# Expert results written to token order by GpSimd, with the place carried in each row (four layers of attention and feed-forward)

## What is computed

```python
x = x + L0_xattn(layernorm(x), ctx, ...)   # convolved causal attention
x = x + L0_ffn(layernorm(x), ...)          # shared expert + 2 of 8 experts, gelu
x = x + L1_xattn(ctx, layernorm(x), ...)   # attention at sampled places
x = x + L1_ffn(layernorm(x), ...)          # 2 of 8 experts, silu gate
x = x + L2_xattn(layernorm(x), ctx, ...)   # cross attention
x = x + L2_ffn(layernorm(x), ...)          # 2 of 8 experts, relu
x = x + L3_xattn(layernorm(x), ctx, ...)   # cross attention
x = x + L3_ffn(layernorm(x), ...)          # product keys, 8 rows per token
```

```python
h = act(xf @ Wfc[e] + bfc[e]) @ Wproj[e] + bproj[e]
routed = routed + h * gate[:, e:e + 1]     # gate is 0 but for two experts a token
```

## Time and profile before

| | |
|---|---|
| median of 3 runs | 1910.25 us |
| the three runs | 1899.67, 1910.25, 1910.5 us |
| profiled execution, its own time | 1902.02 us |
| its span | 1900.3 us |
| busy TensorE, weight load | 1273.0 us (67%), 771.8 us (41%) |
| busy VectorE, ScalarE, GpSimd | 1026.5 (54%), 530.6 (28%), 565.7 us (30%) |
| mean granted TensorE clock | 0.754 |
| blocks of stage 0, 1, 2 | 647 to 740, 1094 to 1194, 1449 to 1543 us |

### The profile page before, as it was taken

One profiled execution on the slowest core, in us unless ns is written; L12 is line 12 of the kernel. 1 busy time (PEld: TensorE's weight loads), 2 busy tenths in 40 slices (PEclk: granted clock), 3 DMA queues, 4 the chain that ended last, 5 costly groups with the idle time before them and its releaser, 6 DMA issues. The chain is left out here.

```text
span 1900.3 us, 26101 instructions
## 1 busy us (share of the span) xinstructions
PE 1273.0 (67%) x9212; PEld 771.8 (41%) x9212; DVE 1026.5 (54%) x2918; ACT 530.6 (28%) x1053; POOL 565.7 (30%) x700
## 2 busy tenths in 40 slices
PE   1458878787884896455645399378876955787720
PEld 1223334343442785345645288222335842222210
DVE  2454455454553232599999655334433325547796
ACT  0123233332341452122312133023423522323310
POOL 6041222212334002541011600331132033155674
PEclk8588798887995998555555599669967978866665
DMA  5930000000003121433532111400001210022232
GB/s 135 389 136 1 1 1 1 1 1 0 12 7 105 41 67 48 119 100 92 136 93 61 34 60 62 130 23 1 12 18 49 67 49 23 2 63 64 79 98 74
DMA packets 73254, 116.48 MB, mean 61 GB/s; under 512 B 11565, under 2 KB 52320, under 8 KB 70624
## 3 DMA queue, kind: packets, MB, share of 16 engines
q1 hardware_dynamic: 60320, 85.24, 14.9%
q0 software_dynamic: 12800, 29.51, 5.4%
HBM read 77.03 MB, written 37.68 MB: 60 GB/s over the span
## 5 line engine op out<-in xcount | busy, mean ns | idle before, releaser
L1671 DVE CUSTOM_DVE_ANT_0 arena<-ps,far 128x512 f32<-128x512 f32 (+3 forms) x256 | 118.2, 488 | 108.6 <-PE ps L1345 107.7
L2002 POOL DMA_INDIRECT wide<-in_w_ud,arena x128 | 130.0, 1015 | 77.7 <-DVE arena L2033 40.7
L2922 PE MATMUL ps<-wide,arena 78*128 78x32 bf16 x3840 | 112.1, 187 | 51.6 <-ACT wide L3035 41.8
L1260 POOL TENSOR_SCALAR_AFFINE_SELECT arena<-arena 128x260 f32<-128x260 f32 (+1 forms) x128 | 53.7, 432 | 308.9 <-ACT arena L1538 308.8
L810 POOL DMA_INDIRECT arena<-ys_d,slot_i x64 | 61.2, 956 | 246.6 <-DMA ys_d<-arena 197.4
L2922 PEld LDWEIGHTS ps<-wide,arena 78*128 78x128 bf16 x3840 | 110.3, 104 | 58.9 <-ACT wide L3035 45.2
L983 PEld LDWEIGHTS ps<-arena 128*128 128x128 f32 (+1 forms) x1012 | 123.4, 192 | 4.0
L983 PE MATMUL ps<-arena 128*128 128x128 f32 (+1 forms) x1012 | 123.6, 275 | 0.0
L1538 ACT ACTIVATE arena<-ps 128x1024 f32<-128x1024 f32 (+1 forms) x96 | 84.6, 881 | 109.9 <-PE ps L1367 109.4
L1367 PE MATMUL ps<-arena 32*128 32x128 f32 (+3 forms) x512 | 114.2, 491 | 1.1 <-DVE arena L1690 1.1
L2543 DVE TENSOR_REDUCE arena<-ps 128x6 f32<-128x462 f32 (+1 forms) x96 | 54.9, 581 | 93.6 <-PE ps L2289 69.9
(11 more groups left out here) (498 smaller groups left out, 2632.4 us busy)
## 6 DMA issues: line engine op xcount, KB each, us to landing
arena<-low_d SPq DMA_DIRECT2D x32, 780.0 KB
xs_d<-zrow SPq DMA_DIRECT2D x1, 10240.0 KB, 30.1
ys_d<-zrow SPq DMA_DIRECT2D x1, 10240.0 KB, 55.9
arena<-xs_d SPq DMA_DIRECT2D x69, 128.0 KB, 2.0
ys_d<-arena SPq DMA_DIRECT2D x69, 128.0 KB, 1.7
arena<-in_w SPq DMA_DIRECT2D x2, 1408.0 KB
wide<-in_Wfc SPq DMA_DIRECT2D x1, 2048.0 KB, 11.8
wide<-in_Wproj SPq DMA_DIRECT2D x8, 256.0 KB, 6.5
```

The source lines that it names most:

```text
L1671: ins = nc.vector.tensor_tensor_reduce(junk[:, n % 2, 384 * i:384 * i + w], ps[:, n % 2, 384 * i:384 * i + w], far[:, T - w:T], 1.0, 3 * N ...
L2002: pool.indirect_dma_start(out=rows_g[t % 4][:, h, :], out_offset=None, in_=A["w_ud"], in_offset=bass.IndirectOffsetOnAxis(ap=eidi[:, t % 8 ...
L2922: mm = nc.tensor.matmul(ps[:, 2 * (i % 3) + h // 2, col:col + 4 * HD], ring[m_ % 4][:, h * NK + p_, t % 2 * P:t % 2 * P + P], table[n // 4 ...
```

## The change

Each row that goes to an expert gets a 129th value, the number of the DRAM row to which its result shall go: 2048 rows for the first choices and 2048 for the second, in token order, behind one row for each of the 5888 slots of the blocks, to which the results of empty slots go. Since the two choices of a token have different numbers, they need two sets of rows in SBUF: `rows` and `twins` (the gated stage had two already). VectorE writes the number's column and, in the plain stages, normalises each batch twice.

In the blocks SyncE no longer stores. VectorE computes from the loaded numbers of block i the targets `goal` (128x2, integer), at the head of result(i); it waits before that until the indirect writes of block i-2 have landed, since `goal` and `yb` have two buffers each. load(i) now waits for goal(i-3) besides turn(i-3). GpSimd waits for each result and writes it with two indirect DMAs of 128 rows (`results`) to `y_d`, which replaces `ys_d` and isn't filled with zeros.

Behind the blocks SyncE waits for all writes and loads the results of each batch with two plain DMAs of 256 KB (`summands`), the last batch's in `last_rows`; two pairs of buffers serve the four batches. VectorE's `combine` adds a batch at a time. The gathers are gone from GpSimd's order. The wide weights for stage 2 are loaded behind the last batch's results of stage 1.

```diff
+RW = D + 1
+TRASH = NBLK * BLK
+STAGE = 16384
 ...
-        ys_d = nc.dram_tensor("ys_d", (SLOTS, D), F32, kind="Internal").ap()
+        xs_d = nc.dram_tensor("xs_d", (SLOTS, RW), F32, kind="Internal").ap()
+        y_d = nc.dram_tensor("y_d", (TRASH + 2 * NTT * P, D), F32, kind="Internal").ap()
 ...
+                nc.vector.tensor_scalar(rows[b][:, :, D], token[:, tiles(b)], float(STAGE * n + NTT * P), None, ALU.add)
+                if not gated:
+                    nc.vector.tensor_scalar(twins[b][:, :, D], token[:, tiles(b)], float(STAGE * n), None, ALU.add)
+                    for t in range(NT):
+                        nc.vector.tensor_scalar(twins[b][:, t, 0:D], xa[:, NT * b + t, :], mv16[:, NT * b + t, 0:1],
+                                                rstd16[:, NT * b + t:NT * b + t + 1], ALU.subtract, ALU.mult)
 ...
                     if i >= 3:
                         sp.wait_ge(m["T"], i - 2)
+                        sp.wait_ge(m["goal"], i - 2)
                     sp.dma_start(xb[:, i % 3, :, :], xs_d[bass.ds(r, BLK), :].rearrange("(p c) d -> p c d", c=2))\
                         .then_inc(m[f"x{i % 3}"], 16)
-                def store(i):
 ...
+                for b in range(B - 1):
+                    summands(sp, b)
+
+            def summands(sp, b):
+                if b >= 2:
+                    sp.wait_ge(m["added"], b - 1)
+                for j in range(2):
+                    lo = TRASH + NTT * P * j + T * b
+                    sp.dma_start(yg[b % 2][j], y_d[lo:lo + T, :].rearrange("(t p) d -> p t d", p=P)).then_inc(m[f"ys{b % 2}"], 16)
+
+            def last_rows(sp):
+                summands(sp, B - 1)
 ...
-            def gather(pool, lo, hi):
-                for t in range(lo, hi):
-                    if t >= 4:
-                        pool.wait_ge(m["added"], t - 3)
-                    for j in range(2):
-                        pool.indirect_dma_start(out=yg[:, t % 4, j, :], out_offset=None, in_=ys_d,
+            def results(pool):
+                for i in range(NBLK):
+                    pool.wait_ge(m["y"], i + 1)
+                    for c in range(2):
+                        pool.indirect_dma_start(out=y_d, in_=yb[:, i % 2, c, :], in_offset=None,
+                                                out_offset=bass.IndirectOffsetOnAxis(ap=goal[:, i % 2, c:c + 1], axis=0))\
+                            .then_inc(landed[i % 2], 16)
 ...
                 def result(i, one):
+                    if i >= 2:
+                        dve.wait_ge(landed[i % 2], sent(i % 2, i // 2))
+                    dve.wait_ge(m[f"x{i % 3}"], 16 * (i // 3 + 1))
+                    nc.vector.scalar_tensor_tensor(goal[:, i % 2, :], xb[:, i % 3, :, D], float(-STAGE * n), trash[:, i, :], ALU.add, ALU.max).then_inc(m["goal"], 1)
                     dve.wait_ge(m["down"], i + 1)
-                    if i >= 2:
-                        dve.wait_ge(m[f"ys{i % 2}"], 16 * (i // 2))
 ...
             def combine(dve, ch, b):
-                for t in range(NT * b, NT * b + NT):
-                    added_to(dve, ch, t)
+                dve.wait_ge(m[f"ys{b % 2}"], 32 * (b // 2 + 1))
                 for j in range(2):
                     if gated:
-                        ins = nc.vector.tensor_tensor(xa[:, t, :], xa[:, t, :], yg[:, t % 4, j, :], ALU.add)
+                        ins = nc.vector.tensor_tensor(x_all[:, b, :, :], x_all[:, b, :, :], yg[b % 2][j], ALU.add)
 ...
                 blocks.settled(pool)
-                blocks.gather(pool, 0, 5)
                 rstd(0)
-                blocks.gather(pool, 5, 8)
 ...
                 rstd(1)
-                blocks.gather(pool, 8, 16)
```

More of the change, by code:

```diff
@@ L36 @@
 NEG = -1e30
-ARENA = 23104
+ARENA = 23500
 STOP = 99
@@ L588, in build @@
         at[0] = 14400
[L589 to L592, removed]
+        late_rows = [[carve(NT, D) for _ in range(2)]]
+        rows2 = [carve(NT, RW) for _ in range(B)]; turned2 = carve(T)
+        late_rows.append([carve(NT, D) for _ in range(2)])
@@ L623, in build, with routing @@
         xa = x_all[:, :, :, :].rearrange("p b t d -> p (b t) d")
-        def routing(n, rows, scaled, turned_to, place, bank, emptied, finished, reuse):
+        def routing(n, rows, twins, turned_to, place, bank, emptied, finished, reuse):
             gated = n == 1
@@ L655, in turn @@
                     pe.wait_ge(r["xn"], NT * b + t + 1)
[L656 removed]
+                    mm = nc.tensor.transpose(ps[:, k_, t * P:t * P + P], rows[b][:, t, 0:D], ident[:, :])
                 mm.then_inc(turn7, 1)
@@ L760, in scatter @@
                 for j in range(2):
-                    src = (scaled if gated and j == 0 else rows)[b]
+                    src = (twins if j == 0 else rows)[b]
                     pool.indirect_dma_start(out=xs_d, in_=src[:, t, :], in_offset=None,
@@ L1046, in emptied @@
                 return i + 1 - d, d
-            R_ = routing(n, rows, None, turned_to, place, bank, emptied, lambda dve, b: None,
+            R_ = routing(n, rows, twins, turned_to, place, bank, emptied, lambda dve, b: None,
                          lambda act, b: act.wait_ge(W["zero"], wcount["zero"]) if b == 3 else None)
@@ L1098, in route_all, with expert_stage @@
             clear_sems(attn_sems + list(r.values()))
-        def expert_stage(n, attention, rows, scaled):
+        def expert_stage(n, attention, rows, twins):
             blocks = moe(n)
@@ L1106, in _ @@
                     blocks.sync(sp)
-                    if parts.sync is not None:
-                        parts.sync(sp)
+                    parts.sync(sp)
                 @block.gpsimd
                 def _(pool):
-                    blocks.gpsimd(pool, rows, scaled)
+                    blocks.gpsimd(pool, rows, twins)
                     if parts.ahead_gpsimd is not None:
                         parts.ahead_gpsimd(pool)
+                    blocks.results(pool)
                     parts.gpsimd(pool, Chain(pool, pool_chain))
@@ L2177, in reuse @@
                     act.wait_ge(turn7, place["lg", b - 1] + 1)
-            R_ = routing(2, rows2, None, lambda b: turned2, place, bank, emptied, finished, reuse) if routes else None
+            R_ = routing(2, rows2, twins2, lambda b: turned2, place, bank, emptied, finished, reuse) if routes else None
             K_ = product_keys(place, emptied, finished) if keys_after else None
@@ L2191, in block_keys, with sync @@
                                         headmask[:, :].unsqueeze(2).to_broadcast([P, H, S2]), ALU.mult).then_inc(c["kbd"], 1)
+            def sync(sp):
+                blocks.last_rows(sp)
+                if keys_after:
+                    K_.store(sp)
             def gpsimd(pool, ch):
@@ L2752, in reuse @@
                 else:
-                    act.wait_ge(m["added"], NTT)
-            R_ = routing(1, rows1, scaled1, lambda b: turned1, place, bank, emptied, finished, reuse)
+                    act.wait_ge(m["added"], B)
+            R_ = routing(1, rows1, twins1, lambda b: turned1, place, bank, emptied, finished, reuse)
             def wrapped(eng, ch, b):
```

135 lines of the change are left out of this document (68 added, 67 removed).

## The result

| | before | after |
|---|---|---|
| median | 1904.97 us (4 runs, 1899.67 to 1910.5) | 1945.85 us (4 runs, 1940.39 to 1948.3) |
| profiled execution, its span | 1902.02, 1900.3 us | 1947.25, 1945.5 us |
| busy TensorE, VectorE, GpSimd | 1273.0, 1026.5, 565.7 us | 1312.4, 1048.5, 599.2 us |
| blocks of stage 0, 1, 2, first transpose to last result | 93.0, 99.2, 93.3 us | 97.9, 152.5, 98.1 us |

The changed kernel takes 1.021 times as long, 95% interval 1.0164 to 1.0257. The forecast of 1934 us lies 12 us under the median, which is inside its range. The medians lie 40.9 us apart. The span of the profiled executions grew by 45.2 us where the sum had 30.

A forecast was written before the change was run, and what follows sets the result against it. No engine was taken as full over the span; TensorE bounds the expert stages. Terms 45 + 5 + 7 - 9 - 18 = +30 us gave 1932 from the profiled 1902.0, adjusted to 1934 us, range 1900 to 1967.

The forecast's parts named there:

- The last step of the sum: From 1932 us, the profiled run plus 30, halfway toward runs whose median lies 8 us higher: forecast 1934 us.
- gated blocks: Gated stage: loads wait for places computed behind the third product; 6.4 us a block for 4.15, 20 blocks, +45 us.
- plain blocks: Plain stages: loads come later, behind the weight copies; 0.25 us per two blocks, +5 us, range 0 to 10.
- routing: Attentions before the stages: second set of rows and narrow operations on VectorE, +7 us, range 4 to 13.
- last result to first statistics: Behind each stage: write, two loads and sums replace the old tail; -9 us together, range -4 to -14.
- first to fourth statistics: Three attentions: third batch's norm no longer waits behind GpSimd's gathers; 7.0, 6.7 and 4.7 us go, -18 us.
- last stretch of the program: The forecast's sum had no term for this stretch, so 0.
- the rival, which the prediction had as a case apart: Gated stage: clock falls to its lower level, 2.8 us more in half of 20 blocks, +28 us: 1962; chance 0.18.
- the clock near 1: Sign of being right: gated stage's TensorE busy share falls to about 65% at a clock near 1.
- whether the copies would hold up GpSimd's writes: Plain stages: by the skill's rule some 0.9 us per block, about 2 us more each stage; left out of the sum.
- The writes' landing: Plain stages: rival where writes land only after 4 us and gate every block, some +10 us each: 1954; chance 0.06.
- "No change" as a rival: Start of three attentions: ending GpSimd's gathers relieves 43 us against costs of 57, time unchanged, 1920; chance 0.22.

The follow-up runs named there:

- the filler: Changed kernel plus seven unused identity transposes a gated block while TensorE waits for rows: 1935.68 us, ratio 1.0185 against the kernel before.
- the kernel with the same extra work alone: Kernel before, with VectorE normalising each batch's rows twice in the plain stages' routing: 1907.27 us, ratio 1.002; on another chip 1928.13 us, 1.0081.
- the order alone changed: Kernel before, with GpSimd computing batch 2's rstd ahead of the gathers of tiles 12 to 15 in both cross attentions: 1891.51 us, ratio 0.996.
- the places early: Changed kernel, with the places of block i+1 computed at the head of VectorE's round i, four buffers: 1876.48 us, ratio 0.9861 against the kernel before.

## Why the prediction was right, and where its terms were off

The direction, the mechanism and its place were right. Each line below is a stretch of the two profiled executions. The size came out by some luck: the costs were 26 us above the forecast, and the reliefs 11 above it, which hid part of that. The last step of the sum also has a slip: halfway between 1932 and 1940 lies 1936 and not 1934.

| term of the sum | forecast | profile |
|---|---|---|
| gated blocks, 99.2 to 152.5 us | +45 | +53.3 |
| plain blocks, 93.0 to 97.9 and 93.3 to 98.1 | +5 | +9.7 |
| routing, first attention 14.9, its end -0.6, sampled 1.3, first cross 4.8 | +7 | +20.4 |
| last result to first statistics, three times | -9 | -14.4 |
| first to fourth statistics, three times | -18 | -18.3 |
| last stretch of the program, 243.3 to 238.0 | 0 | -5.3 |
| sum | +30 | +45.4 |

(The span's difference is 45.2; the rest is rounding and the sampled attention's 48.2 to 48.1.)

- **Gated stage.** The chain was worked out at 6.4 us a block and takes 6.25, so the wait costs 20 blocks 2.1 us each, 42 us in place of 45. The rest came from the rival, which the prediction had as a case apart with 0.18: seven of the blocks take 7.9 us, and 7 x 1.65 = 12 us are the clock, as the filler showed (11.1). The prediction had 2.8 us a block at the lower level, in ten blocks. The two were no alternatives. The prediction judged the clock by a stretch with TensorE busy 6.5 of 10 us at 0.91; that row itself holds a loss, and the stage shows 0.90, not the clock near 1 that was named as a sign of being right. The Trainium skill (TensorE: Matmul & The Clock Gate, HAM oscillation) describes a fall in every tile after longer waits; here waits of 1.9 us stand in every block and the fall came in every third one, so the trace agrees that such waits can cost the clock, and not that they do each time.
- **Plain stages.** 0.25 us per two blocks were forecast, 0.42 more delay for the load and 0.39 more wait were measured, against the rows above. The part that was left out is the weight copy, 0.64 and not 0.42 us. The prediction asked whether the copies would hold up GpSimd's writes, and found no such row: rightly, all 138 writes issued in 0.96 to 1.08 us. It didn't ask the reverse. The Trainium skill (SBUF — State Buffer, Who interferes with whom) says that VectorE in a 2-port mode and GpSimd exclude each other and that whichever issues first blocks the other; by that the copy, issued behind the write, would wait. The trace agrees in part: the second copy, begun 0.54 us into the write, has a median of 642 ns, but the first, begun 0.2 us into the same write, keeps 429. Whether the copies run in a 2-port mode no run shows, so the lengthening is measured and its cause is open. The writes' landing (2.2 us median) held no block; VectorE waited for it once, 0.3 us.
- **Routing.** The term sized worst: 9 us of VectorE time in attentions taken at a third, because VectorE is about half busy there. The profile shows 20 us, 15 of them in the first attention, where the granted clock was 0.75 and not 0.84; a term for the clock was missing. What makes it fall there no run shows. The times of the kernel with the same extra work alone show between none and 15, and the 4.8 us of the first cross attention may as well come from its earlier start behind the stage.
- **Behind the stages.** -14.4 and not -9. In the gated stage, from the last result's end (1255.73) to the load took 5.0 us against 5.5, and from the load to the first sum 3.8 against 4.9.
- **Third batch.** The waits went as foreseen, to 0.52 us. With the order alone changed, the two waits of 13.7 us in the cross attentions were worth 7.6 us by the ratio and 11.4 by the medians; in the profile the first cross attention gives its share back at a lower clock.
- **"No change" as a rival.** It needed reliefs of 38 us. They came to 38.0 us in the profile (14.4 + 18.3 + 5.3), but the costs to 83 and not 57. The 5.3 are no shown relief: the last stretch takes 237.8 to 243.4 us in five profiles in which it is unedited, the kernel before among them. With the places early the reliefs stay and most costs go, which is why that version is faster than the kernel before.

## What to carry to other kernels

When a buffer is freed by two readers, the later one in its engine's order sets the load: give the second reader a place ahead of the work that the first one's successors wait for, and enough buffers for its own result, before judging the idea. Here computing one 0.15 us operation a block earlier, ahead of the three products and with four buffers for it, was worth 66 us by the ratios, and turned a kernel 2.1% slower into one 1.4% faster. The wait per block cost its length and, in every third block, the clock of what followed; price both together, not as alternatives. Where several engines take turns, a few us in one profile of one attention say little; compare the stretches of several profiles with the medians.

## What the runs showed of the hardware

- Seven transposes a block in TensorE's idle time, results unused, raised the stage's granted clock from 0.90 to 0.98 and shortened it by 11.1 us.
- The clock over a long stretch of an attention differs with the work the same: 361 matmuls of the first cross attention ran at 0.82 to 0.84, in 101.8 to 102.3 us, in three profiles, and at 0.75 in 109.5 us in one where they began 7 us earlier. With twice the normalisation they took 92.7 us at 0.95 and 108.7 at 0.79 in two profiles of one kernel, whose first attention had 0.76 and 0.83.
- A VectorE copy of 128x512 takes 0.42 to 0.43 us alone and when it begins 0.2 us into a GpSimd indirect write of results, and 0.64 when it begins 0.54 us into one, while the write keeps its 0.96.
- An indirect write of 128 rows of 512 bytes landed 2.2 us after its issue (median of 138), a plain load of 256 KB of results in 3.2 us (median of 16).
